# Mamba scan kernel: D*xc as a ScalarE copy added by accumulating transposes, and delta products of two channel tiles on different TensorE rows

## The chip, the core and the metric

The kernel runs on one core of a Trainium2 chip. Five engines work side by side and meet at semaphores: TensorE (PE, with its weight loads shown as PEld), VectorE (DVE), ScalarE (ACT), GpSimd (POOL) and SyncE (SP, which issues DMAs here). The metric is the time of one execution on the device, in microseconds (us); lower is better.

## The reference, cut to what matters

A token tower of three parts: embedding with attention, a bidirectional Mamba block, and a low-rank feed-forward layer. The change lies in the Mamba block, which is computed twice, once for each direction:

```
xh, z  = split(x @ in_w.T)
xc     = silu(conv_b + sum over 4 taps of shifted xh * conv_w)
proj   = xc @ xproj_w.T                   # 16 dt, 16 B and 16 C rows
delta  = softplus(proj.dt @ dt_w.T + dt_b)
h      = exp(delta * A) * h + (delta * xc) * B        # scan over time, 16 states
y      = (sum over states of h * C  +  xc * D) * silu(z)
out    = y @ out_w.T
```

There are 512 channels (four channel tiles of 128), 16 states, two sequences of 2048 tokens, and everything here is float32.

## The kernel before, in words

The function `mamba` cuts the tokens of both sequences and both directions into chunks of 512: 16 steps (`STEPS`). A step is 64 tiles, numbered k = 4n + i for state n and channel tile i. For every tile, in this order of data:

- ACT makes two arrays: `bu` (L1233, the product of the transposed delta*xc with B, needed some tiles ahead) and `da` (L1248, exp(delta*A)).
- PE transposes the tile of `bu` into PSUM: `inject`, L1118, four transposes into `ps_x`, of which there are two buffers (`NX` = 2). So inject t waits for scan t-2.
- DVE runs the scan (L1322) over 512 tokens and writes `hs`. After each fourth scan of a step that is not the last of its sequence it keeps the carry (L1327).
- POOL multiplies by C (L1047) and writes `g`.
- PE adds `g` into `ps_y` by accumulating transposes (`add`, L1130), four tiles later (`LAG` = 4). So slot k of PE is: inject k, add k-4, and then what the table puts there.

Everything that the next step needs is put between these tiles by tables written by hand. `PE_FROM`, `ACT_AT` and `DVE_AT` give, for each engine, the tile k after which it does a piece of step s+1: the input products XH (L1065), the convolution CONV (L1082, L1087), PROJ (L1092), the transposes of B, BT (L1096), the delta products DELTA (L1100), the gated output's transposes YT (L1074), Z (L1068), and the transposes of delta*xc, DUT (L1106). All of these go through two PSUM banks in turn (`ps_a`, `NA` = 2), in the order of `sequence`: XH, CONV, PROJ, BT, DELTA 0 to 3, YT 0 to 3, Z 0, DUT 0 to 3, Z 1 to 3. A piece may start only when the piece two before it has been read out of its bank. ACT reads out all but CONV and DELTA, which DVE reads. On ACT, entry 27 is the silu of xc and z with two table loads (L1192, L1197, L1213); PROJ is read out after tile 35, BT after tile 37. Softplus comes in halves of two channel tiles: DVE caps (L1272, "cap"), ACT takes exp and ln (L1203, L1205), DVE joins (L1279, "join"). DUT is fed by POOL's four products delta*xc (`make_du`, L1034), after tile `DU_AT`.

D*xc is added in the slots of state `SKIP_AT` = 5, which is PE slots 24 to 27 with the lag: a product of xc with a diagonal matrix `skips` of D, 128 columns each, four for a tile (L1136). `skips` is made once on DVE (L1306), as the diagonal matrices `taps` are (L1303).

`weight_transposes`, early in the program, lays out the weights in DRAM with their rows where the step wants them. The proj rows lie at partitions 0 (dt), 32 (B) and 64 (C).

Each engine works its own list in order, so an instruction that waits holds all that is behind it.

Of the kernel before, what the change touches and what calls it, by code (L numbers as in the profile page):

```python
# [857 lines left out]
def mamba(nc, sem, dirs, win_scr, xp_scr, dtw_scr, xn_scr, y_scr, c_scr):  # L858

    with ExitStack() as ctx:  # L860
# [68 lines left out]
        def evacuated(eng, f):  # L929
# [26 lines left out]
        DU_AT = 44
        GATE_AT = 2

        with nc.Block() as block:
            @block.sync  # L960
            def _(sp):
# [33 lines left out]
                for z, w in enumerate(dirs):  # L995
# [594 lines left out]
```

## Time and profile before

| what | value |
|---|---|
| median of 3 runs | 3946.2 us (3939.92 to 3947.28) |
| the profiled execution, its own time | 3942.12 us |
| its span | 3940.3 us |
| PE busy | 3642.9 us (92%) |
| DVE busy | 2970.8 us (75%) |
| ACT busy | 2765.8 us (70%) |
| POOL busy | 1451.6 us (37%) |

Attention and projections come first, the Mamba block runs from about 1800 us to 3621 us, and the feed-forward layer ends the program. The busy shares are of the whole span; in the Mamba block all four engines are busy most of the time, so what counts is who waits for whom at each place of a step. Matmul records overlap their neighbours, so a busy PE may still have room.

In what follows, T is the start of scan 24 of the step that begins near 2108 us: T = 2151.54 us. "T+16.8" is 16.8 us after it. The other steps have the same pattern.

### The profile page before, as it was taken

The page shows a single profiled execution, that of the slowest core. Times are in us where ns is not written, and L with a number is a line of the kernel's source. Part 1 is how long each engine was busy: PE and PEld are TensorE (multiplying, and loading weights), DVE is VectorE, ACT ScalarE, POOL GpSimd, SP SyncE. Part 2 cuts the span into 40 slices and gives each one's busy share as a digit, 9 for nine tenths or more (in the row PEclk, how much of TensorE's full clock was granted, in tenths as well). Part 3 has the DMA queues.
Part 4 walks back from the last instruction along what each step waited for, and adds up shares of the span by engine and source line. Part 5 has one row for each costly group of instructions (what it writes and reads, how often), then busy time and mean ns, then how long its engine had stood idle before and what let it go on. Part 6 is the DMA issues. An engine that isn't in the chain of part 4 may idle for free. (4 is left out here: it accounts for less than half of the span.)

```text
span 3940.3 us, 64166 instructions
## 1 busy us (share of the span) xinstructions
PE 3642.9 (92%) x20577; PEld 1970.5 (50%) x20577; DVE 2970.8 (75%) x3944; ACT 2765.8 (70%) x3830; POOL 1451.6 (37%) x1284
## 2 busy tenths in 40 slices
PE   7699999999999999945899999999999999996999
PEld 4223333233323333222677767777777777775554
DVE  5799999899989999333778888888888888886111
ACT  2246666666666666812888999999888989996232
POOL 3000000000000000000677877777777877786000
PEclk9789999999999999977999999999999999998999
DMA  5510101010100100042011111111111111113221
GB/s 136 150 42 4 41 4 41 4 42 16 30 22 23 38 7 4 5 138 81 33 44 55 60 55 55 59 63 53 52 47 54 60 55 55 49 55 102 81 92 49
DMA packets 121702, 202.32 MB, mean 51 GB/s; under 512 B 25392, under 2 KB 68368, under 8 KB 121456
## 3 DMA queue, kind: packets, MB, share of 16 engines
q1 hardware_dynamic: 101264, 173.97, 13.7%
q10 hardware_dynamic: 18656, 20.85, 1.7%
q0 software_dynamic: 1536, 4.20, 0.7%
q8 instruction: 158, 2.59, 0.3%
q14 instruction: 88, 0.72, 0.1%
HBM read 147.83 MB, written 50.72 MB: 50 GB/s over the span
## 5 line engine op out<-in xcount | busy, mean ns | idle before, releaser
L1047 POOL TENSOR_TENSOR m_g<-m_hs,m_cb 128x512 f32<-128x512 f32 x1024 | 1295.4, 1280 | 379.3 <-DVE m_hs L1322 376.3
L661 DVE TENSOR_REDUCE a_mx<-a_ps_m 128x1 f32<-128x512 f32 x2048 | 1311.8, 686 | 156.4 <-PE a_ps_m L520 139.2
L632 ACT ACTIVATE a_probs<-a_ps_s 128x1024 f32<-128x1024 f32 x1024 | 995.0, 1020 | 466.5 <-PE a_ps_s L557 465.9
L1322 DVE TENSOR_TENSOR_SCAN m_hs<-m_da,m_carry,m_ps_x 128x512 f32<-128x512 f32 x768 | 967.8, 1274 | 177.8 <-PE m_ps_x L1118 157.1
L1248 ACT ACTIVATE m_da<-m_delta,m_a_cur 128x512 f32<-128x512 f32 x1024 | 734.0, 717 | 102.1 <-DVE m_hs L1322 101.2
L520 PE MATMUL a_ps_m<-a_k,a_q 112*128 112x512 bf16 x2048 | 732.0, 394 | 41.9 <-DMA a_q<-q_scr 26.5
L1233 ACT ACTIVATE m_bu<-m_dut,m_bt 128x512 f32<-128x512 f32 x1024 | 730.8, 714 | 0.2
L1118 PEld LDWEIGHTS m_ps_x<-m_ident,m_bu 128*128 128x128 f32 x4096 | 494.6, 144 | 383.4 <-issue 302.0
L1118 PE MATMUL m_ps_x<-m_ident,m_bu 128*128 128x128 f32 x4096 | 635.0, 278 | 41.8 <-DVE m_hs L1322 28.8
L1130 PE MATMUL m_ps_y<-m_ident,m_g 128*128 128x128 f32 x4096 | 625.5, 276 | 14.0 <-POOL m_g L1047 14.0
L557 PE MATMUL a_ps_s<-a_q,a_k 115*128 115x512 bf16 (+1 forms) x2048 | 611.3, 381 | 1.4
L534 PE MATMUL a_ps_o<-a_probs,a_v 128*32 128x512 f32 x4096 | 546.4, 605 | 0.7 <-ACT a_probs L632 0.7
L520 PEld LDWEIGHTS a_ps_m<-a_k,a_q 112*128 112x128 bf16 (+1 forms) x2048 | 200.0, 98 | 670.9 <-DVE a_mx L661 271.0
L480 POOL CAST a_neg_parts<-a_neg 128x16 bf16<-128x16 f32 x32 | 6.3, 196 | 1411.8 <-DVE a_neg L664 1411.8
L1130 PEld LDWEIGHTS m_ps_y<-m_ident,m_g 128*128 128x128 f32 x4096 | 487.4, 143 | 18.8 <-POOL m_g L1047 18.3
L1322 DVE TENSOR_TENSOR_SCAN m_hs<-m_da,m_ps_x 128x512 f32<-128x512 f32 x256 | 309.7, 1216 | 99.4 <-PE m_ps_x L1118 73.9
L557 PEld LDWEIGHTS a_ps_s<-a_q,a_k 115*128 115x128 bf16 x2048 | 195.3, 98 | 216.4 <-ACT a_probs L632 39.3
L1082 PE MATMUL m_ps_a<-m_xh,m_taps 128*128 128x512 f32 (+3 forms) x512 | 260.2, 595 | 2.4 <-ACT m_xh L1173 2.4
L534 PEld LDWEIGHTS a_ps_o<-a_probs,a_v 128*32 128x32 f32 x4096 | 80.7, 108 | 207.3 <-issue 197.8
L1065 PE MATMUL m_ps_a<-m_xn,m_win 128*128 128x512 f32 x256 | 133.7, 609 | 24.1 <-DVE m_skips L1306 23.6
L1068 PE MATMUL m_ps_a<-m_win,m_xn 128*128 128x512 f32 x256 | 135.8, 617 | 6.6 <-DVE m_delta L1279 3.8
L1489 ACT ACTIVATE ffn_hid<-ffn_ps_g,ffn_b 128x512 f32<-128x512 f32 x64 | 43.2, 686 | 134.2 <-PE ffn_ps_g L1451 134.1
(154 smaller groups left out, 2461.4 us busy)
## 6 DMA issues: line engine op xcount, KB each, us to landing
m_cb<-c_scr SPq DMA_DIRECT2D x128, 512.0 KB, 3.7
y_scr<-m_ysb SPq DMA_DIRECT2D x16, 1024.0 KB, 6.7
ffn_y<-y_scr SPq DMA_DIRECT2D x16, 1024.0 KB, 10.2
a_k<-k_scr SPq DMA_DIRECT2D x224, 64.0 KB, 2.2
a_q<-q_scr SPq DMA_DIRECT2D x224, 64.0 KB, 2.6
m_xn<-xn_scr SPq DMA_DIRECT2D x16, 512.0 KB, 5.1
q_scr<-p_partsq SPq DMA_DIRECT2D x24, 256.0 KB, 2.4
k_scr<-p_partsk SPq DMA_DIRECT2D x24, 256.0 KB, 2.6
```

The lines of the kernel that those rows point to most:

```text
L520: nc.tensor.matmul(bank(i), q_st[0:KQ, buf, bass.ds(c, 1), h, st * P:(st + 1) * P].rearrange("p c n -> p (c n)"), k_st[0:KQ, buf, h, tc * ...
L534: last = nc.tensor.matmul(ps_o[h * VW:(h + 1) * VW, :], v_st[:, buf, t, h], probs[:, t % 2, h], start=t == 0, stop=t == NT - 1)
L557: last = nc.tensor.matmul(ps_s[half][:, i], k_st[0:KQM, buf, 2 * half + i, t * P:(t + 1) * P], q_st[0:KQM, buf, bass.ds(c, 1), 2 * half + ...
L632: nc.scalar.activation(probs[:, t % 2, 2 * half:2 * half + 2], ps_s[half][:, :, :], ACT.Exp, scale=float(DK) ** -0.5).then_inc(exped, 1)
L661: nc.vector.reduce_max(mx[:, i // NC, i % NC:i % NC + 1], bank(i), AX.X).then_inc(m_maxed, 1)
L1047: nc.gpsimd.tensor_tensor(g[:, t % NG], hs[:, t % NHS], cb[:, quarter % 2, n % CQ], ALU.mult).then_inc(g_ok, 1)
L1082: last = nc.tensor.matmul(bank[:, here], taps[:, z, dt, DC - 1 - back], xh[:, dt, there], start=first, stop=final and p == 0)
L1118: last = nc.tensor.transpose(ps_x[:, t % NX, tb * P:(tb + 1) * P], bu[:, (s * DS + n) % NBU, tb, i * P:(i + 1) * P], ident[:, :])
L1130: last = nc.tensor.matmul(ps_y[:, i, tb * P:(tb + 1) * P], g[:, t % NG, tb * P:(tb + 1) * P], ident[:, :], is_transpose=True, start=n == 0 ...
L1233: nc.scalar.activation(bu[:, m % NBU, tb], dut[:, s % 2, tb], ACT.Copy, scale=bt[:, s % 2, tb, n:n + 1]).then_inc(bt_ok, 1)
L1248: nc.scalar.activation(da[:, t % NDA], delta[:, q, i], ACT.Exp, scale=a_cur[:, z, i, n:n + 1]).then_inc(da_ok, 1)
L1322: nc.vector.tensor_tensor_scan(hs[:, t % NHS, rev], da[:, t % NDA, rev], ps_x[:, t % NX, rev], carry[:, n, i:i + 1] if p else 0.0, ALU.mul ...
```

## The change

- D*xc: ACT multiplies xc of the current step by the column D into a new buffer `skip`, one ACTIVATE of 128x512 after each of tiles 38 to 41 (`SCALE_AT`). PE adds it to `ps_y` with accumulating transposes against the identity, four for a tile, in the slots of state 10 (`SKIP_AT` = 10), which is PE slots 44 to 47. Slots 24 to 27 hold nothing any more. `skips` and its DVE work go away; ACT waits for `skipped` before it overwrites the buffer, PE for `skip_ok`.
- Delta products: the dt rows of proj are made twice, at partitions 0 and 96, and dt_w is loaded twice, at the same partitions. Channel tiles 0 and 2 use rows 0 to 15, tiles 1 and 3 rows 96 to 111. The products are issued in pairs, in slots 36 and 41; before, they stood in 34, 35, 40 and 41.
- Moved with them: caps from tiles 34, 35, 40, 41 to 36, 37, 41, 42; joins from 37, 38, 43, 44 to 39, 40, 44, 45; `DU_AT` from 44 to 45; softplus from 39 and 45 to 40 and 46; YT from slots 44-47 to 45-48; Z 0 from 48 to 49; DUT from 50-53 to 51-54; the other Z by one slot. ACT's read-outs of YT stay at 48 to 51 and that of Z 0 at 53, those of DUT move from 54-57 to 55-58, Z 1 to 3 stay.
- Two more small weight DMAs before the first step (the wait on them goes from 14 to 16), eight more small ACT copies in `weight_transposes`, and the first conv waits for one count less.

```
-                   28: PROJ, 33: BT, 34: DELTA, 35: DELTA + 1, 40: DELTA + 2, 41: DELTA + 3,
-                   44: YT, 45: YT + 1, 46: YT + 2, 47: YT + 3, 48: Z,
+                   28: PROJ, 33: BT, 36: DELTA, 41: DELTA + 2,
+                   45: YT, 46: YT + 1, 47: YT + 2, 48: YT + 3, 49: Z,
...
-        SKIP_AT = 5
+        SKIP_AT = 10
+        SCALE_AT = 38
...
-                  27: SILU, 35: PROJ, 37: BT, 39: SOFTPLUS, 45: SOFTPLUS + 1,
+                  27: SILU, 35: PROJ, 37: BT, 40: SOFTPLUS, 46: SOFTPLUS + 1,
...
-                        last = nc.tensor.matmul(bank, wdt[:, z, dt * P:(dt + 1) * P], proj[X_DT:X_DT + R, q], start=True, stop=True)
+                        rows = slice(X_DT2, X_DT2 + R) if dt % 2 else slice(X_DT, X_DT + R)
+                        last = nc.tensor.matmul(bank, wdt[rows, z, dt * P:(dt + 1) * P], proj[rows, q], start=True, stop=True)
...
                     if n == SKIP_AT:
+                        pe.wait_ge(skip_ok, s * ND + i + 1)
                         for tb in range(NTB):
-                            nc.tensor.matmul(ps_y[:, i, tb * P:(tb + 1) * P], xc[:, s % 2, i, tb * P:(tb + 1) * P], skips[:, where(s)[0], i],
-                                             start=False, stop=False)
+                            last = nc.tensor.matmul(ps_y[:, i, tb * P:(tb + 1) * P], skip[:, i, tb * P:(tb + 1) * P], ident[:, :],
+                                                    is_transpose=True, start=False, stop=False)
+                        last.then_inc(skipped, 1)
...
                     if t < LAST and k in PE_AT and (s + 1, PE_AT[k][0]) in number:
                         fill(s + 1, *PE_AT[k])
+                        if PE_AT[k][0] in (DELTA, DELTA + 2):
+                            fill(s + 1, PE_AT[k][0] + 1, 0)
...
+                def scale_skip(s, i):
+                    if s and i == 0:
+                        act.wait_ge(skipped, s * ND)
+                    nc.scalar.activation(skip[:, i], xc[:, s % 2, i], ACT.Copy, scale=cols[:, where(s)[0], 2, i:i + 1]).then_inc(skip_ok, 1)
```

On PE, slots 33 to 37 of a step before, from inject 33 on:

```order
L1118 MATMUL m_ps_x<-m_ident,m_bu 128x128 x4
L1130 MATMUL m_ps_y<-m_ident,m_g 128x128 x4
L1096 MATMUL m_ps_a<-m_ident,m_proj 128x16 x4
L1118 MATMUL m_ps_x<-m_ident,m_bu 128x128 x4
L1130 MATMUL m_ps_y<-m_ident,m_g 128x128 x4
L1100 MATMUL m_ps_a<-m_proj,m_wdt 128x512
L1118 MATMUL m_ps_x<-m_ident,m_bu 128x128 x4
L1130 MATMUL m_ps_y<-m_ident,m_g 128x128 x4
L1100 MATMUL m_ps_a<-m_proj,m_wdt 128x512
```

And now, where L1122 is inject, L1134 add, L1099 BT and L1104 the delta products:

```order
L1122 MATMUL m_ps_x<-m_ident,m_bu 128x128 x4
L1134 MATMUL m_ps_y<-m_ident,m_g 128x128 x4
L1099 MATMUL m_ps_a<-m_ident,m_proj 128x16 x4
L1122 MATMUL m_ps_x<-m_ident,m_bu 128x128 x4
L1134 MATMUL m_ps_y<-m_ident,m_g 128x128 x4
L1122 MATMUL m_ps_x<-m_ident,m_bu 128x128 x4
L1134 MATMUL m_ps_y<-m_ident,m_g 128x128 x4
L1122 MATMUL m_ps_x<-m_ident,m_bu 128x128 x4
L1134 MATMUL m_ps_y<-m_ident,m_g 128x128 x4
L1104 MATMUL m_ps_a<-m_proj,m_wdt 128x512 x2
```

BT stays in slot 33; the first two delta products leave slots 34 and 35 and stand together in slot 36.

On ACT, from the read-out of BT after tile 37 on, before:

```order
L1183 ACTIVATE m_bt<-m_ps_a 128x64
L1233 ACTIVATE m_bu<-m_dut,m_bt 128x512
L1248 ACTIVATE m_da<-m_delta,m_a_cur 128x512
L1233 ACTIVATE m_bu<-m_dut,m_bt 128x512
L1248 ACTIVATE m_da<-m_delta,m_a_cur 128x512
L1203 ACTIVATE m_delta<-m_delta 128x1024
L1205 ACTIVATE m_delta<-m_delta 128x1024
```

And now, where L1247 is `bu`, L1262 `da`, L1238 the new copy, L1211 and L1213 exp and ln of softplus:

```order
L1191 ACTIVATE m_bt<-m_ps_a 128x64
L1247 ACTIVATE m_bu<-m_dut,m_bt 128x512
L1262 ACTIVATE m_da<-m_delta,m_a_cur 128x512
L1238 ACTIVATE m_skip<-m_xc,m_cols 128x512
L1247 ACTIVATE m_bu<-m_dut,m_bt 128x512
L1262 ACTIVATE m_da<-m_delta,m_a_cur 128x512
L1238 ACTIVATE m_skip<-m_xc,m_cols 128x512
L1247 ACTIVATE m_bu<-m_dut,m_bt 128x512
L1262 ACTIVATE m_da<-m_delta,m_a_cur 128x512
L1238 ACTIVATE m_skip<-m_xc,m_cols 128x512
L1211 ACTIVATE m_delta<-m_delta 128x1024
L1213 ACTIVATE m_delta<-m_delta 128x1024
```

Three copies and one more pair of `bu` and `da` stand ahead of the first softplus; the fourth copy comes after the next pair.

On PE, slots 44 to 46 now, where L1141 is the new addition of `skip` and L1077 is YT:

```order
L1122 MATMUL m_ps_x<-m_ident,m_bu 128x128 x4
L1134 MATMUL m_ps_y<-m_ident,m_g 128x128 x4
L1141 MATMUL m_ps_y<-m_ident,m_skip 128x128 x4
L1122 MATMUL m_ps_x<-m_ident,m_bu 128x128 x4
L1134 MATMUL m_ps_y<-m_ident,m_g 128x128 x4
L1141 MATMUL m_ps_y<-m_ident,m_skip 128x128 x4
L1077 MATMUL m_ps_a<-m_ident,m_zs 128x128 x4
L1122 MATMUL m_ps_x<-m_ident,m_bu 128x128 x4
L1134 MATMUL m_ps_y<-m_ident,m_g 128x128 x4
L1141 MATMUL m_ps_y<-m_ident,m_skip 128x128 x4
L1077 MATMUL m_ps_a<-m_ident,m_zs 128x128 x4
```

Before, each of slots 44 to 47 held inject, add and one YT.

## Rows read from the trace of the kernel before

**Rows 1.** Group of the BT transposes: busy us, mean ns | idle before, releaser

```profile
L1096 PE MATMUL m_ps_a<-m_ident,m_proj 16*128 16x16 f32 x64 | 6.2, 207 | 9.9 <-ACT m_proj L1181 9.9
```

**Rows 2.** Timeline of ACT in one step: start, duration, instruction, idle before

```profile
2151.66 1.91 ACT L1192 ACTIVATE m_xc<-m_xc 128x2048 f32<-128x2048 f32 x1 [0.93 <-DVE m_xc L1263]
...
2156.69 0.72 ACT L1233 ACTIVATE m_bu<-m_dut,m_bt 128x512 f32<-128x512 f32 x1
...
2166.51 0.57 ACT L1181 ACTIVATE m_proj<-m_ps_a 80x512 f32<-80x512 f32 x1
...
2170.16 0.71 ACT L1248 ACTIVATE m_da<-m_delta,m_a_cur 128x512 f32<-128x512 f32 x1
...
2182.61 1.06 ACT L1203 ACTIVATE m_delta<-m_delta 128x1024 f32<-128x1024 f32 x1 [0.47 <-DVE m_delta L1272]
2183.70 1.07 ACT L1205 ACTIVATE m_delta<-m_delta 128x1024 f32<-128x1024 f32 x1
...
2196.38 0.59 ACT L1185 ACTIVATE m_zs<-m_ps_a 128x512 f32<-128x512 f32 x1
...
2201.50 0.60 ACT L1187 ACTIVATE m_dut<-m_ps_a 128x512 f32<-128x512 f32 x1
```

**Rows 3.** Timeline of DVE in the same step

```profile
2151.54 1.27 DVE L1322 TENSOR_TENSOR_SCAN m_hs<-m_da,m_carry,m_ps_x 128x512 f32<-128x512 f32 x1
...
2168.34 1.28 DVE L1322 TENSOR_TENSOR_SCAN m_hs<-m_da,m_carry,m_ps_x 128x512 f32<-128x512 f32 x1 [0.43 <-ACT m_da L1248]
...
2185.05 0.74 DVE L1279 SCALAR_TENSOR_TENSOR m_delta<-m_ps_a,m_cols,m_delta 128x512 f32<-128x512 f32 x1
...
2187.54 3.96 DVE L1322 TENSOR_TENSOR_SCAN m_hs<-m_da,m_carry,m_ps_x 128x512 f32<-128x512 f32 x3
...
2212.52 3.62 DVE L1322 TENSOR_TENSOR_SCAN m_hs<-m_da,m_carry,m_ps_x 128x512 f32<-128x512 f32 x3 [0.26 <-PE m_ps_x L1118]
```

**Rows 4.** Timeline of PE in the same step

```profile
2167.23 0.39 PE L1096 MATMUL m_ps_a<-m_ident,m_proj 16*128 16x16 f32 x4 [0.60 <-ACT m_proj L1181]
...
2168.57 1.12 PE L1100 MATMUL m_ps_a<-m_proj,m_wdt 16*128 16x512 f32 x2
2169.63 0.66 PE L1118 MATMUL m_ps_x<-m_ident,m_bu 128*128 128x128 f32 x4
...
2194.63 0.66 PE L1130 MATMUL m_ps_y<-m_ident,m_g 128*128 128x128 f32 x4 [0.68 <-POOL m_g L1047]
...
2202.15 1.13 PE L1068 MATMUL m_ps_a<-m_win,m_xn 128*128 128x512 f32 x2
```

**Rows 5.** Timeline of POOL in the same step

```profile
2188.36 4.98 POOL L1034 TENSOR_TENSOR m_du<-m_delta,m_xc 128x512 f32<-128x512 f32 x4
```

**Rows 6.** Timeline of PE before the first step: BT and a delta product side by side

```profile
1848.47 0.69 PE L1100 MATMUL m_ps_a<-m_proj,m_wdt 16*128 16x512 f32 x1
1848.52 0.33 PE L1096 MATMUL m_ps_a<-m_ident,m_proj 16*128 16x16 f32 x3
```

**Rows 7.** Timeline of all engines: making of the diagonal matrices and PE's first product

```profile
1810.43 0.42 SPq L1002 DMA_DIRECT2D m_wdt<-dtw_scr  x1
...
1816.40 3.22 DVE L1303 TENSOR_SCALAR m_taps<-m_ident,m_conv_w 128x128 f32<-128x128 f32 x16
1816.73 6.73 PE L1065 MATMUL m_ps_a<-m_xn,m_win 128*128 128x512 f32 x9 [23.61 <-DVE m_skips L1306]
```

**Rows 8.** Timeline of all engines in the last step, slots 24 to 28

```profile
3558.96 1.06 PE L1136 MATMUL m_ps_y<-m_skips,m_xc 128*128 128x128 f32 x8
...
3560.73 1.06 PE L1136 MATMUL m_ps_y<-m_skips,m_xc 128*128 128x128 f32 x8
...
3564.53 0.71 ACT L1248 ACTIVATE m_da<-m_delta,m_a_cur 128x512 f32<-128x512 f32 x1
...
3565.89 7.14 DVE L1322 TENSOR_TENSOR_SCAN m_hs<-m_da,m_carry,m_ps_x 128x512 f32<-128x512 f32 x6 [0.49 <-PE m_ps_x L1118]
```

**Rows 9.** Busy time and granted clock over slots 42 to 53 (PEclk before the DMA share)

```profile
2182.00:2202.00 20.00, 17.04 (x134) 14.54 (x132) 17.25 (x19) 19.49 (x34) 18.66 (x16) 1.00 0.22 74
```

More of the change, by code:

```diff
@@ L34 @@
 ND = DI // P
-X_DT, X_B, X_C = 0, 32, 64
-XPW = X_C + DS
+X_DT, X_B, X_C, X_DT2 = 0, 32, 64, 96
+XPW = X_DT2 + R
 FF, RK = 1024, 64
@@ L880, in mamba @@
         wxp = sb("wxp", [P, 2, ND, XPW], FP32)
-        wdt = sb("wdt", [R, 2, DI], FP32)
+        wdt = sb("wdt", [XPW, 2, DI], FP32)
         conv_w = sb("conv_w", [P, 2, ND, DC], FP32)
@@ L885, in mamba @@
         taps = sb("taps", [P, 2, ND, DC, P], FP32)
-        skips = sb("skips", [P, 2, ND, P], FP32)
+        skip = sb("skip", [P, ND, CH], FP32)
         xn = sb("xn", [P, 2, KD, CH], FP32)
@@ L917, in mamba @@
         stored = s_("stored")
+        skip_ok, skipped = s_("skip_ok"), s_("skipped")
         XH, CONV, YT, PROJ, BT, DELTA, Z, DUT = 0, 4, 8, 12, 13, 14, 18, 22
@@ L941, in mamba @@
                    8: CONV, 12: CONV + 1, 16: CONV + 2, 20: CONV + 3,
-                   28: PROJ, 33: BT, 34: DELTA, 35: DELTA + 1, 40: DELTA + 2, 41: DELTA + 3,
-                   44: YT, 45: YT + 1, 46: YT + 2, 47: YT + 3, 48: Z,
-                   50: DUT, 51: DUT + 1, 52: DUT + 2, 53: DUT + 3, 54: Z + 1, 56: Z + 2, 58: Z + 3}
+                   28: PROJ, 33: BT, 36: DELTA, 41: DELTA + 2,
+                   45: YT, 46: YT + 1, 47: YT + 2, 48: YT + 3, 49: Z,
+                   51: DUT, 52: DUT + 1, 53: DUT + 2, 54: DUT + 3, 55: Z + 1, 57: Z + 2, 59: Z + 3}
         PE_AT = {k + part: (j, part) for k, j in PE_FROM.items() for part in range(parts[j])}
-        SKIP_AT = 5
+        SKIP_AT = 10
+        SCALE_AT = 38
         SILU, SOFTPLUS = FILLS, FILLS + 1
         ACT_AT = {5: XH, 7: XH + 1, 9: XH + 2, 11: XH + 3,
-                  27: SILU, 35: PROJ, 37: BT, 39: SOFTPLUS, 45: SOFTPLUS + 1,
+                  27: SILU, 35: PROJ, 37: BT, 40: SOFTPLUS, 46: SOFTPLUS + 1,
                   48: YT, 49: YT + 1, 50: YT + 2, 51: YT + 3, 53: Z,
-                  54: DUT, 55: DUT + 1, 56: DUT + 2, 57: DUT + 3, 59: Z + 1, 61: Z + 2, 63: Z + 3}
+                  55: DUT, 56: DUT + 1, 57: DUT + 2, 58: DUT + 3, 59: Z + 1, 61: Z + 2, 63: Z + 3}
         JOIN = FILLS
         DVE_AT = {11: CONV, 15: CONV + 1, 19: CONV + 2, 23: CONV + 3,
-                  34: DELTA, 35: DELTA + 1, 37: JOIN, 38: JOIN + 1,
-                  40: DELTA + 2, 41: DELTA + 3, 43: JOIN + 2, 44: JOIN + 3}
-        DU_AT = 44
+                  36: DELTA, 37: DELTA + 1, 39: JOIN, 40: JOIN + 1,
+                  41: DELTA + 2, 42: DELTA + 3, 44: JOIN + 2, 45: JOIN + 3}
+        DU_AT = 45
         GATE_AT = 2
@@ L1001, in _ @@
                     sp.dma_start(wxp[:, z], xp_scr[z]).then_inc(w_in, 16)
-                    sp.dma_start(wdt[:, z], dtw_scr[z]).then_inc(w_in, 16)
+                    for first in (X_DT, X_DT2):
+                        sp.dma_start(wdt[first:first + R, z], dtw_scr[z]).then_inc(w_in, 16)
                 load_xn(1)
@@ L1248, in _ @@
                     nc.scalar.activation(da[:, t % NDA], delta[:, q, i], ACT.Exp, scale=a_cur[:, z, i, n:n + 1]).then_inc(da_ok, 1)
+                    if SCALE_AT <= k < SCALE_AT + ND:
+                        scale_skip(s, k - SCALE_AT)
                     if k in ACT_AT:
@@ L1303, in _ @@
                             last = nc.vector.tensor_scalar(taps[:, z, dt, tap], ident[:, :], conv_w[:, z, dt, tap:tap + 1], None, ALU.mult)
-                    last.then_inc(taps_ok, 1)
-                    for dt in range(ND):
-                        last = nc.vector.tensor_scalar(skips[:, z, dt], ident[:, :], cols[:, z, 2, dt:dt + 1], None, ALU.mult)
                     last.then_inc(taps_ok, 1)
```

10 lines of the change are left out of this document (5 added, 5 removed).

## Prediction

> **What bounds the kernel now.** I read the timeline of one step engine by engine, then the waits by line, then the windows. Times are from T = 2151.54, the start of scan 24 [rows 3]. The reader is to see three stretches. Up to slot 31 PE sets the pace wherever its slot holds a full product. From T on ACT is on a chain of its own: its silu starts when DVE hands over xc (T+0.12), its first `bu` behind the table loads at T+5.15, and the read-out of PROJ after eight pairs of `bu` and `da` at T+14.97 [rows 2]. None of these shows a wait between; a pair takes (2166.51 - 2156.69) / 8 = 1.23 us, one instruction 0.61. PE's BT waits for just that read-out, 0.60 us here and 9.9 us over the 16 steps [rows 1, 4]. It starts at T+15.69, inject 34 stands behind it, and scan 34 starts at T+16.80 [rows 3]. So at slot 33 the time is ACT's, not PE's. From there to scan 45 (T+36.0) DVE has caps, joins and scans, with softplus on ACT in between: the second exp starts at T+31.07, its ln ends at T+33.23, and join 2 at T+33.51 is just behind it [rows 2, 3]. Then POOL makes du for 4.98 us [rows 5], and add 45 on PE waits for it until T+43.09 [rows 4]. After that PE's Z products set the pace to the end of the step; only the last few tiles run at the scans' 3.62 / 3 = 1.21 us [rows 3].
>
> **The skip leaves slots 24 to 27.** A slot with the skip products lasts 3560.73 - 3558.96 = 1.77 us [rows 8]; without them inject and add remain, about half of that, so PE sheds some 0.89 x 4 = 3.6 us and the scans of these tiles can go at 1.21. But BT and everything behind it waits for the read-out of PROJ at T+14.97, and ACT's list from T to there is unchanged. What PE and DVE gain turns into a longer wait at BT: 0.60 us becomes about 3 us. Worth at scan 34: nothing.
>
> **The delta products.** In slot 34 before, the product and its surroundings take from T+17.03 to the next inject at T+18.09, 1.06 us [rows 4]. Before the first step a delta product (rows 0 to 15) begins at 1848.47 and three BT transposes (rows 32 to 47) at 1848.52, while it runs [rows 6], so products on different rows can overlap. A pair then costs between 1.06 us (full overlap) and 1.06 + 0.86 = 1.92 us (none; 0.86 is half of a 1.77 us slot less a little). I take overlap, for the row shows two row groups at work together. The Trainium skill (TensorEngine Tiling, "Key Properties") says that a change of tiling mode drains TensorE and that tiles run independently. By it half of the entries into the narrow mode fall away besides. The same two overlapping rows agree with its second half. None of it is worth much here: with slots 34 and 35 free the scans 34 to 36 come sooner, but caps and joins are the same in number and are moved two tiles later, and what decides next is softplus on ACT.
>
> **The copies on ACT.** Each reads and writes SBUF with a scale per partition, as `bu` does, so I take 0.61 us; the low bound is 0.50, since a read-out's record is 0.11 to 0.12 shorter than that of `bu` (0.60 against 0.72 [rows 2]). ACT's list: `da` 38 at T+18.62 as before [rows 2], then itself, three copies and two pairs, 0.61 x 8 = 4.9, so the first exp starts at T+23.5; exp and ln 2.1; then the fourth copy and six pairs, 0.61 + 7.4 = 8.0, so the second exp starts at T+33.6 and its ln ends 2.16 us later, T+35.8. Before it was T+33.23. ACT shows no wait in this but those for caps, which DVE now has ready: the copies eat the spare time that the 0.47 us wait at the second exp still shows [rows 2], and the later place of the entry adds a pair. Join 2 must wait for the ln, so it starts at T+35.8 instead of T+33.5: 2.3 us later. Join 2, a scan and join 3 take 2187.54 - 2185.05 = 2.49 us [rows 3], so scan 46 starts at T+38.3; before, scan 45 stood there at T+36.0. One tile more is done, worth 1.2 us: **1.1 us lost**.
>
> **Behind join 3.** du starts after join 3 and POOL's current tile, so add 46 waits until T+43.1 + 2.3 = T+45.4. Before that PE has the four skip transposes more, 4 x 0.44 = 1.8 us (0.44 is a quarter of a slot of 1.77); in slots 46 and 47 they lie in what was the 0.68 us wait for POOL and in POOL's later start: no cost. From add 46 on PE has the list that it had from add 45 on, with one tile fewer at the end: the 1.1 us stands. But the read-outs on ACT are late too. Z 0's stays at tile 53, though its product moved a slot: filled about 1.5 us after add 46 (the rest of the add and a product of 1.1 us), T+46.9, while ACT is there at T+44.84 + 2.5 - 1.2 = T+46.1. From Z 0's read-out to the end of DUT 2's ACT took 2202.10 - 2196.38 = 5.7 us [rows 2] and has now one pair more, 6.9 us: T+53.8. The Z 1 product needs that bank. Before, it started at T+50.61, 0.05 us after the read-out ended at T+50.56 [rows 2, 4], so there is no slack; PE would want it at T+50.6 + 2.3 = T+52.9. **0.9 to 1.0 us lost**, in slots 53 to 55. Nothing behind gives it back, since PE sets the pace there.
>
> **The sum.** A step that prepares the next loses 1.1 + 1.0 = 2.1 us, and there are 15: 31 us. Once, at the start: PE's first product waits for the diagonals [rows 7]; it must now see all 32 `taps`, where it saw 16 and the four `skips`: 12 more of 3.22 / 16 = 0.2, 2.4 us. The two added DMAs cost SP about 0.42 us each ahead of that [rows 7]: 0.9. The eight small copies in the weight preparation cost between nothing and 8 x 0.57 (the read-out of PROJ [rows 2]); each writes 16 columns a row, so I take 1. The last step has no fills: `da` 28 starts 1.36 us before its scan [rows 8], 0.7 of which it needs itself, so 2.5 us of copies cost about 1.8; the lighter slots 24 to 27 give up to 4 x (1.77 - 1.21) = 2.2 back. I take 0, within 2 either way. Together 31 + 2.4 + 0.9 + 1 = 35 us on the profiled execution's 3942.1: 3977. The median of the runs is 4 us over that execution, so I write 3979. Without overlap in the pair the first exp and all behind it come some 0.4 us later a step, 3985. With copies of 0.50 a step loses 0.45 less, 3972.
>
> **The rivals.** (A) *PE's time counts.* If slot 33 were PE's and not ACT's, a step would save 3.6 - 1.8 on the skip and 2 x 1.06 on the delta pairs, 3.9 us; 15 x 3.9 = 59 us, 3887 to 3891. For it: PE is busy 17.04 of 20 us even over slots 42 to 53 [rows 9]. Against it: the wait of BT for ACT in every step [rows 1]. (B) *ACT keeps up.* If the caps, joins and read-outs are not held by ACT (softplus is earlier because xc or BT is), the loss by ln and by the read-outs goes and DVE's path alone counts: about 0 to 0.4 us a step, 3946 to 3954. (C) *The clock falls.* PE will idle 3 us at BT, and the light slots 24 to 27 come before. If the granted clock fell to 1.2 GHz there, inject 34 and the delta pair behind it would take double, some 0.44 + 1.06 in each step: 15 x 1.2 = 18 us more, 3997. Against: PEclk is 1.00 over 20 us of nearly nothing but transposes, with PE idle for 3 us of them [rows 9]. The Trainium skill (TensorE: Matmul & The Clock Gate, "Part 4: PE-mode transpose") says that transposes do not count as activity for the clock; it speaks against trading products for transposes. By that rule slots 44 to 47 would run at 1.2 GHz, and the four skip transposes and their neighbours would take double, within the price of C. The window of rows 9 goes against the rule.
>
> **How the numbers follow.** The forecast, slower by 25 to 50 us with or without full overlap of the pair: 0.64. C: 0.11. B: 0.12. A or part of it: 0.13. The likeliest gives 3979. The range reaches from 3942 (the lower edge of B) to 4000 (the upper edge of C); some 0.15 lies below it, mostly A, and 0.04 above. Within 0.2% means 3938 to 3954, about what a measurement of this kernel can tell from no change. Slower by over that: 0.64 + 0.11 = 0.75; within: 0.12; faster: 0.13.
>
> **What would show it.** The wait of BT for ACT's read-out of PROJ: from 9.9 us in total to some 45. Scan 34 at T+16.8 as before. The wait of join 2 for ln: about 0.7 us in each step, where there was none. New waits of PE for ACT's read-outs of DUT, near 1 us a step. POOL's wait no longer on the path if PE is late. A new step would be some 2 us longer. If scan 34 starts near T+14.7, the reading of slot 33 is wrong and A follows; if join 2 finds its ln ready, the ACT chain is wrong and B follows; a PEclk under 0.97 over the Mamba block speaks for C.

## The result, and the profile after

| kernel | median us (runs) | ratio to before, 95% interval |
|---|---|---|
| before | 3943.29 (3939.92 to 3947.28) | 1 |
| after | 3982.8 (3980.26 to 3984.5) | 1.0099 [1.0082, 1.0117] |

The change costs 39.5 us. The head and the busy shares of the page of after:

```profile
span 3981.0 us, 63720 instructions
...
PE 3630.0 (91%) x20321; PEld 1964.7 (49%) x20321; DVE 2965.2 (74%) x3936; ACT 2805.9 (70%) x3902; POOL 1450.3 (36%) x1284
```

The shares say little: PE has 13 us less to do and ACT 40 us more, over a span that is 40.7 us longer (3981.0 against 3940.3). The groups by line say more. First the BT transposes, then the copies, then the weight loads of DUT (busy us, mean ns | idle before, releaser):

```profile
L1099 PE MATMUL m_ps_a<-m_ident,m_proj 16*128 16x16 f32 x64 | 6.4, 210 | 33.8 <-ACT m_proj L1189 33.8
...
L1238 ACT ACTIVATE m_skip<-m_xc,m_cols 128x512 f32<-128x512 f32 x64 | 45.6, 712 | 0.0
...
L1110 PEld LDWEIGHTS m_ps_a<-m_ident,m_du 128*128 128x128 f32 x256 | 30.0, 147 | 14.7 <-ACT m_dut L1195 11.1 <-issue 3.5
```

Against [rows 1], PE's wait for the read-out of PROJ went from 9.9 to 33.8 us. PE waits for ACT's read-outs of DUT, 11.1 us, where the same row of before reads:

```profile
L1106 PEld LDWEIGHTS m_ps_a<-m_ident,m_du 128*128 128x128 f32 x256 | 31.5, 148 | 3.9 <-issue 3.5 <-ACT m_dut L1187 0.2
```

A mean of 712 ns for a copy is a record, which overlaps its neighbour; in the list a copy costs what it moves the next start by, 0.61 us.

The same step as in rows 2 to 4, one engine after the other. Its T, called T', is 2156.99. PE of after (start, duration, instruction, idle before):

```profile
2172.67 0.39 PE L1099 MATMUL m_ps_a<-m_ident,m_proj 16*128 16x16 f32 x4 [2.17 <-ACT m_proj L1189]
2172.99 1.00 PE L1122 MATMUL m_ps_x<-m_ident,m_bu 128*128 128x128 f32 x4
...
2177.43 1.13 PE L1104 MATMUL m_ps_a<-m_proj,m_wdt 16*128 16x512 f32 x4
...
2208.58 0.66 PE L1110 MATMUL m_ps_a<-m_ident,m_du 128*128 128x128 f32 x4
...
2210.29 0.66 PE L1110 MATMUL m_ps_a<-m_ident,m_du 128*128 128x128 f32 x4 [0.18 <-ACT m_dut L1195]
...
2212.00 1.13 PE L1071 MATMUL m_ps_a<-m_win,m_xn 128*128 128x512 f32 x2 [0.18 <-ACT m_dut L1195]
```

BT waits 2.17 us, and the inject behind it takes 1.00 us where one takes 0.60 to 0.66. The pair of delta products, four records, takes 1.13 us. DUT 2, DUT 3 and Z 1 come 1.71 us apart, where the three lots of transposes from one to the next take 3 x 0.44 = 1.3.

ACT of after: the read-out of PROJ, the first copy, the first exp, the second exp and its ln:

```profile
2171.95 0.58 ACT L1189 ACTIVATE m_proj<-m_ps_a 112x512 f32<-112x512 f32 x1
...
2176.21 0.72 ACT L1238 ACTIVATE m_skip<-m_xc,m_cols 128x512 f32<-128x512 f32 x1
...
2181.27 1.06 ACT L1211 ACTIVATE m_delta<-m_delta 128x1024 f32<-128x1024 f32 x1 [0.67 <-DVE m_delta L1288]
...
2191.29 1.04 ACT L1211 ACTIVATE m_delta<-m_delta 128x1024 f32<-128x1024 f32 x1
2192.37 1.06 ACT L1213 ACTIVATE m_delta<-m_delta 128x1024 f32<-128x1024 f32 x1
```

And DVE: scan 34, then join 2, right behind the ln:

```profile
2174.12 1.28 DVE L1335 TENSOR_TENSOR_SCAN m_hs<-m_da,m_carry,m_ps_x 128x512 f32<-128x512 f32 x1 [2.35 <-PE m_ps_x L1122]
...
2193.76 0.72 DVE L1295 SCALAR_TENSOR_TENSOR m_delta<-m_ps_a,m_cols,m_delta 128x512 f32<-128x512 f32 x1
```

Scan 34 stands at T'+17.1 (before T+16.8), the second exp at T'+34.3 (T+31.07), join 2 at T'+36.8 (T+33.51).

What had not been forecast shows in the windows over the Mamba block, before and then after (length; busy of PE, PEld, DVE, ACT, POOL; PEclk; DMA share; GB/s):

```profile
1880.00:3625.00 1745.00, 1654.33 (x10748) 1254.46 (x10748) 1449.89 (x1460) 1575.94 (x2455) 1368.88 (x1084) 0.99 0.16 53
```

```profile
1880.00:3625.00 1745.00, 1613.66 (x10258) 1222.88 (x10257) 1415.66 (x1433) 1589.12 (x2475) 1337.59 (x1061) 0.97 0.15 52
```

The granted clock is 0.97 in place of 0.99. In the 12 us behind BT it is 1.00 before and 0.86 after:

```profile
2167.50:2179.50 12.00, 10.86 (x69) 7.44 (x69) 11.30 (x14) 11.43 (x19) 9.00 (x8) 1.00 0.13 43
```

```profile
2173.10:2185.10 12.00, 10.84 (x69) 9.05 (x70) 10.41 (x12) 11.30 (x19) 7.80 (x7) 0.86 0.00 2
```

### The profile page after: what moved, and what is told of

It is laid out like the page before. It is cut to its first block and busy times, and to the rows that moved or that the text cites. A ratio compares the mean times of both kernels' runs of the same rounds, so it can differ in the third digit from the quotient of the medians.

```text
span 3981.0 us, 63720 instructions
## 1 busy us (share of the span) xinstructions
PE 3630.0 (91%) x20321; PEld 1964.7 (49%) x20321; DVE 2965.2 (74%) x3936; ACT 2805.9 (70%) x3902; POOL 1450.3 (36%) x1284
## 5 line engine op out<-in xcount | busy, mean ns | idle before, releaser
L1262 ACT ACTIVATE m_da<-m_delta,m_a_cur 128x512 f32<-128x512 f32 x1024 | 730.6, 714 | 100.7 <-DVE m_hs L1335 99.9
L1247 ACT ACTIVATE m_bu<-m_dut,m_bt 128x512 f32<-128x512 f32 x1024 | 727.7, 711 | 0.2
L1122 PE MATMUL m_ps_x<-m_ident,m_bu 128*128 128x128 f32 x4096 | 650.5, 283 | 58.5 <-DVE m_hs L1335 43.5
L1122 PEld LDWEIGHTS m_ps_x<-m_ident,m_bu 128*128 128x128 f32 x4096 | 506.1, 147 | 389.4 <-issue 312.1
L1134 PE MATMUL m_ps_y<-m_ident,m_g 128*128 128x128 f32 x4096 | 639.2, 280 | 17.8 <-POOL m_g L1050 17.8
L1134 PEld LDWEIGHTS m_ps_y<-m_ident,m_g 128*128 128x128 f32 x4096 | 501.0, 146 | 22.4 <-POOL m_g L1050 22.0
```

The source lines that it names most:

```text
L1122: last = nc.tensor.transpose(ps_x[:, t % NX, tb * P:(tb + 1) * P], bu[:, (s * DS + n) % NBU, tb, i * P:(i + 1) * P], ident[:, :])
L1134: last = nc.tensor.matmul(ps_y[:, i, tb * P:(tb + 1) * P], g[:, t % NG, tb * P:(tb + 1) * P], ident[:, :], is_transpose=True, start=n == 0 ...
L1247: nc.scalar.activation(bu[:, m % NBU, tb], dut[:, s % 2, tb], ACT.Copy, scale=bt[:, s % 2, tb, n:n + 1]).then_inc(bt_ok, 1)
L1262: nc.scalar.activation(da[:, t % NDA], delta[:, q, i], ACT.Exp, scale=a_cur[:, z, i, n:n + 1]).then_inc(da_ok, 1)
```

## Experiments

Each kernel ran beside the kernel before on one chip, three groups in all, with before at 3943.58, 3943.99 and 3942.04 us. A ratio is to before in its own group.

### Each half of the change alone

**Before, without the skip products.** What are slots 24 to 27 worth? (In the code shown, `...` stands for what is left out, within brackets too.)

```
-                    if n == SKIP_AT:
-                        for tb in range(NTB):
-                            nc.tensor.matmul(ps_y[...], xc[...], skips[...], start=False, stop=False)
```

> The kernel before without its skip products: D*xc is left out of the result, nothing else is changed, so TensorE slots 24 to 27 of each step hold inject and add alone. Theory of the prediction (slot 33 belongs to ScalarE): scan 34 still starts 16.8 us after scan 24, the wait of the BT transposes for the read-out of PROJ grows from 9.9 us to 30 to 45 us in all, and the time is 3938 to 3943, the last step alone giving up to 2 us. Rival (TensorE's time counts): 0.89 x 4 = 3.6 us a step, 15 steps, 3943 - 54 = 3889, and the wait at BT stays under 15 us.

Measured: 3982.36 us, ratio 1.0096 [1.0079, 1.0113]: neither forecast. Taking 64 groups of products away from PE, and nothing else, costs 39 us. PE of this kernel at BT:

```profile
2168.85 0.39 PE L1096 MATMUL m_ps_a<-m_ident,m_proj 16*128 16x16 f32 x4 [2.18 <-ACT m_proj L1177]
2169.17 1.00 PE L1118 MATMUL m_ps_x<-m_ident,m_bu 128*128 128x128 f32 x4
2169.97 1.06 PE L1130 MATMUL m_ps_y<-m_ident,m_g 128*128 128x128 f32 x4
2170.95 2.07 PE L1100 MATMUL m_ps_a<-m_proj,m_wdt 16*128 16x512 f32 x2
```

and the 12 us behind it:

```profile
2169.40:2181.40 12.00, 11.76 (x46) 7.88 (x45) 7.09 (x8) 7.94 (x13) 4.03 (x5) 0.58 0.01 3
```

The reading of slot 33 holds: scan 34 gains nothing, and the wait at BT grows from 0.60 to 2.18 us. What neither forecast had is behind it. A delta product takes 2.07 us here and 1.12 in [rows 4]. A mean clock of 0.58 over 12 us means the lower level, 1.2 GHz, for 10 of them, and PE gets through 46 matmul records where before has 69. The clock falls here in 14 of the 15 steps that prepare a next one.

**The new skip alone**, in the old tables (tables and single delta products of before, copies after tiles 38 to 41, additions in state 10).

```
-        SKIP_AT = 5
+        SKIP_AT = 10
+        SCALE_AT = 38
...
+                            last = nc.tensor.matmul(ps_y[...], skip[...], ident[:, :], is_transpose=True, start=False, stop=False)
```

> The skip half of the change alone: copies on ScalarE after tiles 38 to 41, added in slots 44 to 47; all delta products use rows 0 to 15 and every table stands as before. ScalarE theory: two copies delay the first softplus by 0.6 us and all four the second by 1.3 us, so join 2 comes about 1.0 us late, the read-outs of DUT another 0.3 us: 1.3 us a step, 20 us, and 3 us at the start: 3966. Rival (the clock: each long wait at BT halves TensorE's clock for a while): most of the change's 39.5 us already here, 3975 or more. Rival (TensorE's time counts): faster than 3943.

Measured: 3992.11 us, 1.0126 [1.0107, 1.0144], and PEclk 0.96 over the block. This is what the rival on the clock gave (3975 or more). The new skip is most of the cost, and in the old tables it costs more than with the pairs.

**The pairs alone**, with the new tables and the old skip products in slots 24 to 27.

```
+                   28: PROJ, 33: BT, 36: DELTA, 41: DELTA + 2,
...
+                        if PE_AT[k][0] in (DELTA, DELTA + 2):
+                            fill(s + 1, PE_AT[k][0] + 1, 0)
```

> The delta half alone: products in pairs on two row groups with the new tables (softplus, caps, joins, YT, DUT one or two tiles later), the skip as TensorE products in slots 24 to 27 as before, no copies. If the later places cost, since the first exp waits for the cap of tile 37 near 24 us and six pairs of bu and da follow: ln ends about 35.4 us after scan 24 and a step loses 1.6 us, 3943 + 24 + 4 = 3971. If the copies on ScalarE are what costs: 3943 to 3950.

Measured: 3952.59 us, 1.0021 [1.0012, 1.0031], between the two forecasts. PEclk is 0.99. The DUT row of this kernel:

```profile
L1110 PEld LDWEIGHTS m_ps_a<-m_ident,m_du 128*128 128x128 f32 x256 | 29.6, 146 | 15.6 <-ACT m_dut L1193 11.9 <-issue 3.5
```

The wait for ACT's read-outs is here without any copy on ACT. So it comes from the table, which reads DUT out a tile later, and not from ACT being late. It amounts to 11.9 us here and 6.5 more ahead of Z 1, 18.4 together. The median is only 9 us up, but that is an average over steps with different clocks: in a step in which neither kernel's clock falls, this kernel takes 1.2 us more than before (the table below), 15 x 1.2 = 18 us, all of the wait. So no gain from the pairs is shown.

**The copies earlier**, on the changed kernel:

```
-        SCALE_AT = 38
+        SCALE_AT = 16
```

> The kernel after with its four ScalarE copies moved from tiles 38 to 41 to tiles 16 to 19, where ScalarE runs some 8 us ahead and waits; everything else as after. If the copies behind tile 37 carry the loss, the second ln ends 2.4 us earlier and the time is near 3983 - 30 = 3953. If the first exp waits for its cap anyway (it showed 0.67 us of such a wait in the profile after), only the fourth copy's 0.61 us and the part of the read-outs go: 0.6 to 1.0 us a step, 3968 to 3974.

Measured: 3973.32 us, 1.0078 [1.0061, 1.0095], as expected. The place of the copies ahead of the two softplus halves costs some 8 to 9 us of the 39; in a step with an undisturbed clock it is 0.9 us (the table below), 13 us in 15 steps.

### Is it the clock?

Two products whose result is overwritten are put ahead of PE's wait at BT, so PE waits less. They add work and take none away. If the time falls all the same, the clock is the likely reason, and the granted clock of each step can be checked.

```
+                        for _ in range(2):
+                            nc.tensor.matmul(bank, win[:, 0, 0:P], xn[:, q, 0], start=True, stop=True)
                         pe.wait_ge(taken, takes[s, PROJ])
```

**In the kernel before without the skip products:**

> The kernel before without its skip products (D*xc left out of the result), with two products of 128x512 added ahead of the wait of the BT transposes; they go into the bank that BT then overwrites and fill TensorE's idle time there. If the 39 us that the removal of the skip products cost come from TensorE's clock falling after a long idle wait, the clock stays at its higher level behind BT and the time goes back to 3940 to 3948 (no gain over before, since slot 33 belongs to ScalarE). If the loss has another cause, the time stays near 3982 or rises by the added products, 15 x 1.7 = 25 us, to 4007.

Measured: 3937.3 us, 0.9986 [0.9976, 0.9996], 45 us less than the same kernel without the filling. BT, the inject behind it and the delta products:

```profile
2163.32 0.41 PE L1098 MATMUL m_ps_a<-m_ident,m_proj 16*128 16x16 f32 x4 [0.37 <-ACT m_proj L1179]
2163.66 0.66 PE L1120 MATMUL m_ps_x<-m_ident,m_bu 128*128 128x128 f32 x4
...
2164.69 1.12 PE L1102 MATMUL m_ps_a<-m_proj,m_wdt 16*128 16x512 f32 x2
```

The wait is 0.37 us in place of 2.18, and the instructions are back at 0.66 and 1.12. So the 39 us of the first experiment were clock: with it held, leaving out the skip altogether is worth 6 us and no more, for slots 24 to 27 are hidden behind ACT's chain. In a step with an undisturbed clock it is worth 0.06 us (the table below), so most of the 6 us comes from elsewhere, likely from steps in which the clock of before itself falls.

**In the changed kernel:**

> The kernel after with the same two products ahead of the wait of BT, nothing else changed. Clock share: the stretches at 1.2 GHz near 16 us behind scan 24 go, and with them about 1 us a step: 3965 to 3972. ScalarE's share alone: the second ln is set by copies and places, nothing changes: 3980 to 3986. Everything is clock: 3950 or less.

Measured: 3973.53 us, 1.0078 [1.0061, 1.0095]. The intervals of the ratios touch, but the runs do not (after from 3980.26, this up to 3976.84), and from first to last scan the trace has 10 us less. The 12 us behind BT:

```profile
2171.70:2183.70 12.00, 10.14 (x70) 7.40 (x70) 11.21 (x13) 11.97 (x21) 8.07 (x8) 1.00 0.01 3
```

The clock is 1.00 again, where after had 0.86. So 9 to 10 us of the change are clock; 3965 to 3972 had been expected, a little too good.

**In the new skip alone:**

> The skip half of the change alone (copies after tiles 38 to 41, added in slots 44 to 47, old tables, delta products unpaired) with the two filling products ahead of BT. Clock as the cause of most of its 48.5 us: back by about 35 us, to 3952 to 3962, the rest being ScalarE's copies (the 1.3 us a step expected before, 20 us, less what the lighter slots give: 6 us) and 3 us at the start. If the copies are the larger part: 3970 or more.

Measured: 3972.12 us, 1.0081 [1.0065, 1.0096]: the worse of the two forecasts. Some 20 us were clock, 30 are not. In an undisturbed step it is 1.2 us over before, where the copies with the new tables cost 0.9. That the softplus stands one tile earlier here and nothing pairs may be why; it was not tested.

**With transposes as filling**, 16 of them in place of the two products, in the kernel before without the skip products:

```
-                        for _ in range(2):
-                            nc.tensor.matmul(bank, win[:, 0, 0:P], xn[:, q, 0], start=True, stop=True)
+                        for _ in range(4):
+                            for tb in range(NTB):
+                                nc.tensor.transpose(bank[...], xc[:, q, 0, ...], ident[:, :])
```

> The kernel before without its skip products (D*xc left out of the result), the idle time ahead of BT filled with 16 transposes of 128x128 in place of the two products of 128x512; about the same 1.7 us of TensorE work. If being busy is what keeps the clock, transposes do as well as products: 3934 to 3942. If transposes do not count as activity for the clock, it falls behind BT as without any filling: 3975 to 3985.

Measured: 3937.88 us, 0.999 [0.9981, 0.9999]. It stands beside 3937.3 with products and 3982.36 without filling.

```profile
2165.07 1.91 PE L1096 MATMUL m_ps_a<-m_ident,m_xc 128*128 128x128 f32 x16
2167.33 0.41 PE L1099 MATMUL m_ps_a<-m_ident,m_proj 16*128 16x16 f32 x4 [0.34 <-ACT m_proj L1180]
```

So float32 transposes held the clock here as well as products did. The Trainium skill (TensorE: Matmul & The Clock Gate, "Part 4: PE-mode transpose") says that they do not count as activity for the clock. For float32 transposes the measurement goes against that, as [rows 9] did.

**The clock step by step.** The traces hold a check that needs no filling. Let the steps be counted from 1, so that the one shown so far is the third, and a step last from its first scan to the first scan of the next. In the change BT waits 1.8 us or more in each of 15 steps, but the clock falls right behind the wait, near T+16, in ten of them only. In the second it does not:

```profile
2061.20:2073.20 12.00, 10.18 (x71) 7.42 (x70) 11.17 (x13) 11.97 (x21) 8.08 (x8) 1.00 0.01 3
```

Against the same steps of the kernel with the clock held, the ten are 0.6 to 1.6 us longer each, 10.1 us together; the other five differ by 0.1 us together. In the kernel without skip products the one step whose clock does not fall is the sixth. It waits 2.17 us too, and takes 109.83 us, as before (109.84) and as with the filling (109.77):

```profile
2447.98:2557.81 109.83, 101.89 (x653) 75.08 (x652) 92.29 (x96) 99.67 (x157) 85.83 (x69) 1.00 0.16 54
```

So the loss stands where the clock falls and nowhere else. But the wait alone does not settle whether it falls, and the kernel before is not free of it: behind its wait of 0.60 us the clock falls near T+20 in five of the 15 steps. Here is the second step, which takes 112.42 us where the kernel without skip products and with the filling takes 109.76:

```profile
2055.30:2067.30 12.00, 11.24 (x54) 8.19 (x55) 9.16 (x11) 9.88 (x17) 6.99 (x7) 0.72 0.11 40
```

With the filling there are four such steps (products) and two (transposes) without the skip, and none in the changed kernel. What decides it in a single step is not shown, and the filling was not tried on the kernel before.

In the seventh step the clock is 1.00 from end to end in many of the kernels. These are before, the pairs alone, the change with the clock held, the same with the DUT read-outs moved back, and the change with both products of a pair on one row group; the sections below tell of the last two:

```profile
2544.62:2654.39 109.77, 104.62 (x685) 78.82 (x684) 92.83 (x96) 99.43 (x156) 85.79 (x69) 1.00 0.19 63
2548.56:2659.54 110.98, 103.31 (x684) 78.31 (x682) 92.89 (x97) 99.58 (x156) 85.82 (x69) 1.00 0.18 59
2556.66:2668.49 111.83, 103.87 (x672) 77.02 (x670) 92.66 (x96) 101.88 (x160) 85.60 (x69) 1.00 0.17 58
2550.28:2660.97 110.69, 103.16 (x672) 77.03 (x670) 92.67 (x97) 101.59 (x160) 85.68 (x69) 1.00 0.18 59
2564.64:2676.84 112.20, 102.97 (x668) 76.74 (x666) 92.66 (x96) 101.99 (x160) 85.59 (x69) 1.00 0.17 58
```

| kernel | undisturbed step, us | over before |
|---|---|---|
| before | 109.77 | |
| without skip products, filled | 109.71 | -0.06 |
| pairs alone | 110.98 | 1.2 |
| change, copies at 16 (sixth step; before 109.84, held 111.90) | 111.04 | 1.2 |
| change, held, DUT read-outs moved back | 110.69 | 0.9 |
| new skip alone, held | 111.01 | 1.2 |
| change, held | 111.83 | 2.06 |
| change, one row group | 112.20 | 2.4 |

The copies cost 0.9 us a step and the new place of the DUT read-outs 1.2, and the two add up to the 2.06 of the change.

### The read-outs of DUT

With the clock held, ACT's read-outs of DUT go back to the tiles of before:

```
-                  55: DUT, 56: DUT + 1, 57: DUT + 2, 58: DUT + 3, 59: Z + 1, 61: Z + 2, 63: Z + 3}
+                  54: DUT, 55: DUT + 1, 56: DUT + 2, 57: DUT + 3, 59: Z + 1, 61: Z + 2, 63: Z + 3}
```

> The kernel after with the filling products ahead of BT and the four read-outs of DUT on ScalarE one tile earlier (54 to 57, as before the change). If PE waits for these read-outs as the prediction says, they come one pair of bu and da, 1.23 us, earlier and a step gains 0.6 to 1.0 us on the 3973.5 us of the held kernel: 3958 to 3965. If the Z products are held by something else: 3972 to 3975.

Measured: 3955.38 us, 1.0034 [1.0022, 1.0046], 18 us under the kernel that it was made from and 3 better than expected. Its row, and the same row of the kernel that it was made from:

```profile
L1112 PEld LDWEIGHTS m_ps_a<-m_ident,m_du 128*128 128x128 f32 x256 | 31.1, 146 | 3.9 <-issue 3.5 <-ACT m_dut L1197 0.2
```

```profile
L1112 PEld LDWEIGHTS m_ps_a<-m_ident,m_du 128*128 128x128 f32 x256 | 29.6, 146 | 15.5 <-ACT m_dut L1197 11.9 <-issue 3.5
```

The waits went, 11.9 us here and 6.5 ahead of Z 1, 18.4 together. 18 / 15 = 1.2 us a step, which is one pair of `bu` and `da` on ACT: just the tile by which the table had moved them.

### The pair on one row group

The changed kernel, with both products of a pair on rows 0 to 15:

```
-                        rows = slice(X_DT2, X_DT2 + R) if dt % 2 else slice(X_DT, X_DT + R)
+                        rows = slice(X_DT, X_DT + R)
```

> The kernel after with both delta products of a pair on rows 0 to 15. Overlap of two row groups worth 0.86 us a pair: the next inject comes that much later behind the first pair, and the time is 0 to 0.8 us a step up, 3983 to 3995. If the overlap is worth nothing on the path: 3983.

Measured: 3992.51 us, 1.0125 [1.0105, 1.0145] (two runs): some 10 us over the change. A pair takes 1.98 us:

```profile
2180.28 1.98 PE L1104 MATMUL m_ps_a<-m_proj,m_wdt 16*128 16x512 f32 x4
```

It is 1.13 us on rows 0 and 96. The two products of a pair do overlap, all but wholly: one alone takes 1.12 us [rows 4]. That is what the Trainium skill says of tiles (TensorEngine Tiling, "Key Properties"), and here the trace agrees.

A step holds two pairs, 1.7 us more in all, of which 0.37 us reach the end of the step (112.20 against 111.83 in the seventh, and 0.37 over the change in the mean of all 15), 5.6 us together. Most of the rest of the 10 us lies outside the steps: in this execution the first scan starts 2.1 us later than in the change, and 1.0 us more passes behind the last.

### Attempts at a better kernel

**The preparation earlier as a whole**, with the copies at 16 (PE, ACT, DVE tables):

```
-                   28: PROJ, 33: BT, 36: DELTA, 41: DELTA + 2,
+                   28: PROJ, 32: BT, 34: DELTA, 39: DELTA + 2,
...
-                  27: SILU, 35: PROJ, 37: BT, 40: SOFTPLUS, 46: SOFTPLUS + 1,
+                  27: SILU, 32: PROJ, 34: BT, 37: SOFTPLUS, 43: SOFTPLUS + 1,
...
-        DU_AT = 45
+        DU_AT = 43
```

> The kernel after with the copies at tiles 16 to 19 and the list behind PROJ moved up: ScalarE reads PROJ out after tile 32 in place of 35 and BT after tile 34, and delta products, caps, joins, softplus, YT, Z and DUT stand two to three tiles earlier than in the change. If slot 33 was held by ScalarE's read-out of PROJ, scan 34 starts near 14.7 us behind scan 24 in place of 16.8, the long idle wait and the clock's fall go too, and a step gains 2 to 3 us on the kernel before: 3895 to 3915. If the freed time is taken back by DUT's read-outs or POOL, 3935 to 3945.

Measured: 3941.51 us, 0.9997 [0.9987, 1.0007]: all of the loss is gone, and there is no gain. The first forecast had scan 34 at T+14.7, and it starts at T+14.9. Scan 35 starts 2.1 us earlier than in the kernel before (T+16.84 against T+18.93), but at scan 61 the two stand level (62.3 and 62.5 us behind T in the mean of 15 steps). In between is a new wait:

```profile
L1110 PEld LDWEIGHTS m_ps_a<-m_ident,m_du 128*128 128x128 f32 x256 | 29.5, 145 | 19.7 <-ACT m_dut L1195 16.1 <-issue 3.5
```

DUT is in slots 49 to 52 and read out after tiles 53 to 56, and PE waits 16.1 us for it, the largest of this row in any kernel here. Read-outs one tile earlier in this kernel were not tried.

**The new skip, old tables, copies at 16, additions in state 8 (slots 36 to 39), clock held**, and one wait at the start shortened:

```
-        SKIP_AT = 5
+        SKIP_AT = 8
+        SCALE_AT = 16
...
-                pe.wait_ge(taps_ok, 2)
+                pe.wait_ge(taps_ok, 1)
```

> Meant to beat both: old tables, unpaired delta products, copies after tiles 16 to 19 where ScalarE waits anyway, skip transposes in slots 36 to 39 where TensorE waits for scans, two filling products ahead of BT, and TensorE's first product waiting for one direction's diagonals only. With nothing of the change's ScalarE load on the chain behind BT it should stand near the held kernel without skip, 3937, less 0.8 us at the start and plus up to 1.8 x 15 = 26 us if slots 36 to 39 have no room: 3934 to 3942. 3950 or more if there is no room.

Measured: 3944.78 us, 1.0006 [0.9997, 1.0015]; 3934 to 3942 had been hoped for. It is as fast as before and no faster: when the copies are off the softplus chain and the clock is held, the new skip costs nothing and gives nothing (109.84 us in the seventh step, before 109.77). No kernel that computes D*xc was shown to be faster than before.

## Why the prediction was right, point by point

The forecast of 3979 us is 4 us under the measured 3982.8, its side and size are right, and so is the chain of reasons for most of it. The clock was left out.

| term | predicted | measured |
|---|---|---|
| start | 4.4 us | first scan at 1885.94, before 1881.95: 4.0 us |
| chain of ACT to join 2, per step | 1.1 us | 0.9 us |
| DUT read-outs, per step | 0.9 to 1.0 us | 1.1 to 1.2 us |
| both, per step | 2.1 us | 2.06 us in an undisturbed step |
| clock, per step | 0 (rival C: 1.2 us) | 10.1 / 15 = 0.7 us |
| last step | 0, within 2 | 0.4 us |

Over all 15 steps the change takes 112.29 us a step and before 109.75, 2.54 more. That is less than 2.06 + 0.7, since before has falls of the clock of its own. 15 x 2.54 + 4.0 + 0.4 = 42.5 us to the last scan; the stretch behind it, which the change does not touch, was 2 us shorter in this execution.

**Slots 24 to 27 are worth nothing: right.** The first experiment with the clock held shows it: 6 us for all of the skip. Scan 34 stands at T'+17.1 against T+16.8. The wait at BT came out at 33.8 us, not 45. PE does not come to BT 2.4 us earlier but 1.6, for its injects now wait for scans on the way, where before had no wait between T and BT:

```profile
2158.41 0.63 PE L1122 MATMUL m_ps_x<-m_ident,m_bu 128*128 128x128 f32 x4 [0.32 <-DVE m_hs L1335]
...
2165.10 0.63 PE L1122 MATMUL m_ps_x<-m_ident,m_bu 128*128 128x128 f32 x4 [0.69 <-DVE m_hs L1335]
```

**The chain on ACT: right.** It can be checked where the clock is held behind BT. That kernel's T is 2155.68. Its two exps and the second ln on ACT, then join 2 and scans 46 and 47 on DVE:

```profile
2179.19 1.04 ACT L1213 ACTIVATE m_delta<-m_delta 128x1024 f32<-128x1024 f32 x1
...
2189.20 1.05 ACT L1213 ACTIVATE m_delta<-m_delta 128x1024 f32<-128x1024 f32 x1
2190.28 1.06 ACT L1215 ACTIVATE m_delta<-m_delta 128x1024 f32<-128x1024 f32 x1
```

```profile
2191.37 0.75 DVE L1297 SCALAR_TENSOR_TENSOR m_delta<-m_ps_a,m_cols,m_delta 128x512 f32<-128x512 f32 x1 [0.38 <-ACT m_delta L1215]
...
2193.86 2.65 DVE L1337 TENSOR_TENSOR_SCAN m_hs<-m_da,m_carry,m_ps_x 128x512 f32<-128x512 f32 x2
```

First exp at T+23.5 (forecast T+23.5), second at T+33.5 (T+33.6), join 2 at T+35.7 behind its ln (T+35.8), the scan behind join 3 at T+38.2 (T+38.3). Join 2 waits 0.38 us here, not 0.7, since a scan before it ends later. In the change itself the clock adds to this: PE's slow stretch behind BT makes the cap late, the first exp waits 0.67 us for it, both exps are 0.8 us later than with the clock held, and join 2 is 1.1 us later (T'+36.8). There join 2 shows no wait for its ln, for it starts behind a late scan; by the prediction's own sign that would have spoken for rival B. The kernel with the clock held is what decides against B.

**1.1 us a step from that chain: nearly right.** An undisturbed step of the held kernel with the DUT read-outs moved back takes 0.9 us more than before, and the copies at tile 16 give just this back (111.90 against 111.04). So the copies make all of it, and the later places of caps, joins and softplus cost nothing by themselves: with the copies at tile 16 a step takes as long as with the pairs alone. The average over all 15 steps would give only 110.41 - 109.75 = 0.66 us; the difference is in steps of before whose clock fell.

**The read-outs of DUT: the mechanism right, its price a little low, and the cause narrower.** The forecast gave 0.9 to 1.0 us and put it on a late ACT and the one pair more. The pairs alone show the wait without copies, and the read-outs moved back remove it whole: it is the tile in the table, 1.2 us, one pair at ACT's pace.

**Overlap of the pair: right, and so is its worth.** Overlap was taken, and no overlap was priced at 0.4 us a step. On one row group a step takes 0.37 us more, and the first exp of the third step starts at T+23.9 instead of T+23.5.

**The clock: the step that failed.** Rival C had the place (behind BT) and the reason (PE idle after thin slots), and was given 0.11, on the strength of [rows 9], where PE idles 3 us in 20 and the clock is 1.00. Those idle times are several short ones, the one at BT is 2.17 us in one piece; whether that is the difference was not tested. Where the clock falls near T+16 it costs 0.6 to 1.6 us, about what C said (1.2), but it falls in ten of the 15 steps, and so costs 10 us and not 18. In the kernel without skip products it falls in 14 steps, for some 10 us in nearly all of these. The test set in the prediction, PEclk under 0.97, was too coarse: it came out at 0.97 in the change, and at 0.96 in the kernel without skip products, where the filling brings back 45 us.

So that the total was hit within 4 us is in part luck. The change loses 10 us to its clock, which the forecast had at nothing. Against that stand some 3 us by which the clock of before itself falls (15 x (2.06 - 1.86), where 1.86 us is what the change with the clock held loses in the mean of all steps) and 2 us behind the last scan.

Rivals A and B are out: scan 34 did not move up, and with the clock held join 2 waits for its ln.

## What to carry to other kernels

Taking work off an engine that then waits for another gains nothing, and if the engine is TensorE it can lose: look at the idle time that the edit makes, and at the granted clock behind it step by step, before counting busy time. A mean of the clock over the whole block hides it. To price one term, compare single steps in which neither kernel's clock fell; averages mix the term with the clock. Where a piece is moved by one slot in a table, price the producer and the reader of its bank separately; here the reader's one tile cost more (18 us) than all new copies (about 9, or 13 by the undisturbed step). Operations added to an engine whose share is only 70% can cost time all the same: four copies of 0.61 us cost 0.9 us a step ahead of the result that the next step waits for, and nothing some twenty tiles earlier.

## What the runs showed of the hardware

- Behind an idle time of about 2.2 us, after slots with eight transposes each, the granted clock fell to 1.2 GHz in most steps: in 14 of 15 without the skip products (0.58 in the mean of the 12 us behind it in the step shown), in ten of 15 in the change (0.86). The same wait without a fall occurs too. With the wait filled down to 0.37 us the clock did not fall there in 11 of 15 steps without the skip products, nor in any of 15 in the change. With 0.60 us, in the kernel before, it fell in five. Removing 64 groups of products so cost 39 us of 3943.
- As filling, 16 float32 transposes held the clock as well as two 512-column products did (3937.88 and 3937.3 us).
- Two float32 products of 16 rows on rows 0 and 96 take 1.13 us together, 1.98 us when both are on rows 0 to 15.
